# Halo of a causal convolution summed in one go, a softplus subtraction and one of sixteen state sums moved off VectorE

## The chip, the cores and the metric

One core of one Trainium2 chip. The metric is the device time in microseconds (us) of one execution, as the median of several runs. Engines are named as the profile names them: PE is TensorE (matmuls and transposes), DVE is VectorE, ACT is ScalarE, POOL is GpSimd, SP is SyncE, whose queue issues all the DMAs of this kernel.

## The reference, cut to what matters

The input is (4, 1024, 512) float32: 4096 tokens, handled in 8 chunks of 512 tokens, two chunks a sequence. Three residual blocks follow each other: half a gated feed-forward, a selective-scan block, half a gated feed-forward.

```python
x = x + 0.5 * ffn(_layernorm(x))
x = x + attn(_layernorm(x))          # W_in, causal conv of 4 taps, silu, Wx, softplus, scan, gate, Wout
x = x + 0.5 * ffn(_layernorm(x))

# inside attn, I = 1024 channels, N = 16 states
conv = causal_conv(h, conv_w)        # 4 taps along time: 3 tokens of the chunk before are needed
h = silu(conv + conv_b)
delta = softplus(dt + dt_bias)
s = exp(d_t * A) * s + d_t * B_t * u_t
y = sum over the 16 states n of s[n] * C_t[n]
```

## The kernel before, in words

**Layout.** Channels lie on the 128 partitions and 512 tokens on the free axis, so that the recurrence of one state over 128 channels is one scan instruction of DVE. The 1024 channels are 8 blocks (`NI`), handled in two groups of 4 (`ig`). Every matmul in float32 is split into a high and a low part (`split`, L499 by ACT for the high part, L500 by DVE or POOL for the low one).

**Stages of a chunk.** `ffn` is the feed-forward (gate and up matmuls L477, tanh L598, two products on DVE L600 and L608, down matmuls L548, `tail`). `prep_in` is the input projection with the convolution: for each block i, ACT writes tap 3 plus the bias from PSUM into `aa` (L652), DVE adds the taps k = 1, 2, 3 of the chunk's own tokens (L659), and where the chunk is the second of its sequence (odd c) each of these is followed by a small DVE operation that adds what tap k takes from the chunk before, 1, 2 or 3 elements wide, from `hsave` (L663). Even chunks save their last three columns into `hsave` (L656). ACT's tanh (L666) and DVE's product (L668) end the block. `softplus` works on two blocks at once (128x1024), in four parts a chunk: ACT computes exp(-abs(x)), 1 plus it, DVE the rounding error of that sum (L792), ACT the logarithm (L794), DVE subtracts the error (L796) and adds max(x, 0) (L800), POOL multiplies by u (L803). `post` reads y back, adds D*u, multiplies by the gate, and projects with Wout; its gate inputs are loaded into 6 slots, 3 of them in `aa`.

**The scan** of chunk c has 32 turns, 16 states n for each of the two groups. In a turn POOL multiplies `dus` by the broadcast row of B in two halves (L892, 128x1024) into one of 3 buffers `sbuf`; ACT computes four exponentials (L906) into 2 PSUM buffers `pa`; DVE runs four scans (L915) over the buffer in place; PE transposes the buffer in four steps tt of four 128x128 blocks (L932) into 2 PSUM banks `pt`; and each bank is multiplied by C and added to `acc` by one DVE operation (L943), apart from state 0, which ACT writes alone (L939). A bank of `pt` is free again when its reader is done, and a buffer of `sbuf` when its transposes are done.

**Order.** All instructions of the kernel are put in streams, and `merge` writes the order of each engine's queue in advance, from a model of durations (`span`) in which the stream that can start first goes first and `RANK` breaks near ties: the transposes and sums are thread T, the products, exponentials and scans are thread S (last in rank), softplus is D, the convolution is C. An engine works off its queue strictly in order, each instruction waiting for its semaphores. The rounds are `ffn1(c)`, `dt1(c-1)`, `post(c-3)` with `scan(c-3)`, `dt2`, `prep_in`, `dt3`, `ffn2(c-3)`, `dt0`, so that scans of older chunks fill the engines beside the projections of newer ones. y goes through memory, so the scan of a chunk isn't tied to its `post`. The weights of this input leave their low parts out in the feed-forwards (the light branch).

Of the kernel before, what the change touches and what calls it, by code (L numbers as in the profile page):

```python
# [7 lines left out]
P = 128  # L8
TC = 512
NCH = 8  # L10
H = 512
NI = 8
N = 16
J = 11
R = 128
HALO = 3
SLOTS = 3
DWELL = 12.0
ISSUE, LAND = 0.42, 2.5
LATE = {"pe": 0.3, "act": 0.08, "dve": 0.08, "pool": 0.1}  # L20
SLACK = 0.3
PEF = 1.0

# [6 lines left out]

RANK = {"z": {}, "l": dict(pe=0, act=0, dve=0, pool=0, slack=SLACK), "c": dict(act=1, dve=1, pool=1, slack=SLACK),
        "m": dict(pe=1, act=1, dve=1, pool=1, slack=SLACK), "d": dict(act=2, dve=2, pool=2, slack=SLACK),
        "t": dict(pe=0, dve=3, act=3), "s": dict(act=4, dve=4, pool=4)}

GU, DN, WIN, WO = 0, 2 * J, 3 * J, 3 * J + 16
NPIECE = 3 * J + 16 + 8
# [2 lines left out]
F32 = mybir.dt.float32  # L39
F32R = mybir.dt.float32r  # L40
ALU = mybir.AluOpType
# [143 lines left out]
def macaron(nc, x_in, wp_in, wx_in, wdt_in, const_in, lnw_in, ds_in, ident_in, out):  # L185
    ctx = ExitStack()
    with ctx:
        def sb(name, shape, dt=F32):
            return ctx.enter_context(nc.sbuf_tensor(name, shape, dt))
# [27 lines left out]
        xT = sb("xT", [P, 2, 4, TC], F32R)  # L217
        act = sb("act", [P, 2, J, TC], F32R)
        th = sb("th", [P, 2, TC])
        aa = sb("aa", [P, 3, TC])  # L220
        hd = sb("hd", [P, 3, TC])
        tb = sb("tb", [P, 8, TC])
        tsT = sb("tsT", [P, 2, TC], F32R)
# [9 lines left out]
        nb = sb("nb", [P, 4])  # L233
        mhalf = sb("mhalf", [P, 12])
        hsave = sb("hsave", [P, NI, 4])
        cst = sb("cst", [P, NCONST])
        csh = sb("csh", [P, 11 + 11 + 4 + 40])
        lnw = sb("lnw", [P, 2 * N])
# [33 lines left out]
        def ld(name, n=1):  # L272
            return [counter(f"{name}{i}") for i in range(n)]
# [1 line left out]
        l_const, l_w, l_wst = ld("l_const"), ld("l_w", SLOTS), ld("l_wst", 4)  # L275
        l_xn, l_x, st_x, st_xn = ld("l_xn")[0], ld("l_x")[0], ld("st_x")[0], ld("st_xn")[0]
        st_u, st_g, st_dl, l_u = ld("st_u", 2), ld("st_g", 2), ld("st_dl")[0], ld("l_u", 5)
        st_b, l_y, l_g = ld("st_b")[0], ld("l_y", 2), ld("l_g", 6)
        l_dl, l_du, l_b, st_y = ld("l_dl", 4), ld("l_du", 4), ld("l_b", 2), ld("st_y", 2)
        l_ud, st_du = ld("l_ud")[0], ld("st_du")[0]  # L280

# [126 lines left out]
        def build(light, first=False):  # L408
# [85 lines left out]
            def freed(name):  # L494
                return free.get(name, ())
# [89 lines left out]
            def ffn(one, c):  # L585
                s_in, s_out = (0, 1) if one else (2, None)
                if first:
                    t_xT = make_xT(t_xn0, tb)
                else:
                    t_xT = make_xT(xn_tok.pop((s_in, c)))  # L590
                    prefetch()
                a_tok = []
                for j in range(J):
                    r, q = j % 3, j % 2
                    slot, t_w = piece(GU + 2 * j)
                    b, w = bank()
                    t = gemm(b, slot, t_w, w, t_xT, 0 if light else None)
                    t_th = M.op("act", lambda e, b=b, q=q, j=j: e.activation(  # L598
                        th[:, q, :], pm[b][:, :], ACT.Tanh, scale=hc(H_GS + j)), t, *freed(("th", q)), table="tanh")
                    t_a = M.op("dve", lambda e, b=b, r=r, q=q: e.scalar_tensor_tensor(  # L600
                        aa[:, r, :], th[:, q, :], 1.0, pm[b][:, :], ALU.add, ALU.mult), t_th, *freed(("aa", r)))
                    free["th", q] = (t_a,)
                    bank_free[b] = (t_a,)
                    if not light:
                        slot, t_w = piece(GU + 2 * j + 1)
                    b, w = bank()
                    t = gemm(b, slot, t_w, w, t_xT, 1 if light else None)
                    t_h = M.op("dve", lambda e, b=b, r=r, j=j: e.scalar_tensor_tensor(  # L608
                        hd[:, r, :], aa[:, r, :], hc(H_US + j), pm[b][:, :], ALU.mult, ALU.mult),
                        t, t_a, *freed(("hd", r)))  # L610
                    bank_free[b] = (t_h,)
                    free["aa", r] = (t_h,)
                    t_hi, t_lo = split(hd[:, r, :], act[:, 0, j, :], act[:, 1, j, :], t_h, lo_eng="pool", waits=freed("act"))
                    free["hd", r] = (t_hi, t_lo)
                    a_tok.append((t_hi, t_lo))
                free["xT"] = (t,)
                if one:
                    tail(J, DN, None, a_tok, x_in, x2_d, 1, c)
                else:
                    tail(J, DN, None, a_tok, x3_d, out, None, c, last_out=True)  # L620
# [14 lines left out]
            def prep_in(c):  # L635
# [5 lines left out]
                    pre_norm(free, ln_out, c + 1)  # L641
                prefetch(0 if c == 0 else 1)
                u_tok, g_tok = [], []
                for i in range(NI):
                    r = i % 2
                    if c == 0 and light and i == NI - SLOTS + 1:
                        split_pieces(later)
                    slot, t_w = piece(WIN + i)
                    b, w = bank()
                    t = gemm(b, slot, t_w, w, t_xT)  # L650
                    cw = lambda k, i=i: hc(H_CW + 4 * i + k)
                    t_c = C.op("act", lambda e, b=b, r=r, i=i, cw=cw: e.activation(  # L652
                        aa[:, r, :], pm[b][:, :], ACT.Identity, bias=hc(H_CB + i), scale=cw(3)),
                        t, *freed(("aa", r)))
                    if even:
                        hs_tok[i] = C.op("dve", lambda e, b=b, i=i: e.tensor_copy(  # L656
                            hsave[:, i, 0:HALO], pm[b][:, TC - HALO:TC]), t_c, n=1)
                    for k in range(1, 4):
                        t_c = C.op("dve", lambda e, b=b, r=r, k=k, cw=cw: e.scalar_tensor_tensor(  # L659
                            aa[:, r, k:TC], pm[b][:, 0:TC - k], cw(3 - k), aa[:, r, k:TC], ALU.mult, ALU.add),  # L660
                            t_c)
                        if not even:
                            t_c = C.op("dve", lambda e, i=i, r=r, k=k, cw=cw: e.scalar_tensor_tensor(  # L663
                                aa[:, r, 0:k], hsave[:, i, HALO - k:HALO], cw(3 - k), aa[:, r, 0:k],
                                ALU.mult, ALU.add), t_c, hs_tok[i], n=1)
                    t_th = C.op("act", lambda e, b=b, r=r: e.activation(pm[b][:, :], aa[:, r, :], ACT.Tanh),  # L666
                                t_c, table="tanh")
                    t_u = C.op("dve", lambda e, b=b, r=r: e.scalar_tensor_tensor(  # L668
                        hd[:, r, :], pm[b][:, :], 1.0, aa[:, r, :], ALU.add, ALU.mult), t_th, *freed(("hd", r)))
                    free["aa", r] = (t_u,)  # L670
                    bank_free[b] = (t_u,)
                    t_hi = C.op("act", lambda e, r=r, i=i: e.activation(act[:, 0, i, :], hd[:, r, :], ACT.Copy),  # L672
                                t_u, *freed("act"))
                    t_lo = C.op("pool", lambda e, r=r, i=i: e.tensor_tensor(  # L674
                        act[:, 1, i, :], hd[:, r, :], act[:, 0, i, :], ALU.subtract), t_hi)
                    t_st = C.dma(st_u[r], u_d[c, i], hd[:, r, :], t_u)
                    u_tok.append(t_st)
                    free["hd", r] = (t_hi, t_lo, t_st)
                    if c and i < NI - 2:
                        g_tok.append(gate(c, i, t_xT))  # L680
# [91 lines left out]
            def softplus(c, part):  # L772
# [11 lines left out]
                if part == 3:  # L784
# [8 lines left out]
                    spw[:, :, :], spw[:, :, :], 1.0, spe[:, :, :], ALU.subtract, ALU.subtract), t_w, n=n)  # L793
                t_l = D.op("act", lambda e: e.activation(spe[:, :, :], spe[:, :, :], ACT.Ln, bias=1.0), t_q,  # L794
                           n=n, table="ln")
                t_l = D.op("dve", lambda e: e.tensor_tensor(spe[:, :, :], spe[:, :, :], spw[:, :, :], ALU.subtract),  # L796
                           t_l, n=n)
                t_u = D.dma(l_ud, spw[:, :, :], u_d[c, i0:i0 + 2].rearrange("k p n -> p k n"),
                            u_tok[i0], u_tok[i0 + 1], t_l)
# [12 lines left out]
            def post(c):  # L812
# [2 lines left out]
                a_tok = []  # L815
                ysb = xT[:, :, :, :].bitcast(F32)
                u_slot = [th[:, q, :] for q in range(2)] + [act[:, 0, k, :].bitcast(F32) for k in range(NI, J)]
                g_slot = [aa[:, q, :] for q in range(3)] + [act[:, 1, k, :].bitcast(F32) for k in range(NI, J)]
                u_free = [freed(("th", q)) for q in range(2)] + [freed("act")] * (J - NI)
                g_free = [freed(("aa", q)) for q in range(3)] + [freed("act")] * (J - NI)  # L820
                t_y = [M.dma(l_y[g], ysb[:, g, :, :], y_d[c * TC:(c + 1) * TC, g * 512:(g + 1) * 512].rearrange(
                    "(t p) n -> p t n", p=P), y_tok[g], *freed("xT")) for g in range(2)]
                for i in range(NI):
                    r, q, v = i % 3, i % 5, i % 6
                    t_u = M.dma(l_u[q], u_slot[q], u_d[c, i], u_tok[i], *u_free[q])
                    t_g = M.dma(l_g[v], g_slot[v], sg_d[c, i], g_tok[i], *g_free[v])
                    b, w = bank()
# [14 lines left out]
                free["xT"] = (t,)  # L842
                for q in range(2):
                    free["th", q] = u_free[q]
                for q in range(3):
                    free["aa", q] = g_free[q]
                tail(NI, WO, 0.5, a_tok, x2_d, x3_d, 2, c)

# [5 lines left out]
            def sf(name):  # L854
                return sfree.get(name, ())
# [5 lines left out]
            def scan(c):  # L861
# [22 lines left out]
                for g in range(2 * N):  # L884
# [43 lines left out]
                    for tt in range(4):  # L928
# [13 lines left out]
                        else:  # L942
                            f = lambda e, tt=tt, a=a, c=c, pb=pb, n=n: e.scalar_tensor_tensor(  # L943
                                a, pt[pb][:, :], cT[:, c % 4, tt, n:n + 1], a, ALU.mult, ALU.add)
                            w = sf(("accw", ig, tt))
                        t_a = T.op("act" if n == 0 else "dve", f, t_t, t_ct, *w)
                        sfree["accw", ig, tt] = (t_a,)
                        sfree["pt", pb] = (t_a,)
                    sfree["sb", s3] = (t_t, t_c)
                    if n == N - 1:  # L950
                        t_s = T.dma(st_y[ig], y_d[c * TC:(c + 1) * TC, ig * 512:(ig + 1) * 512].rearrange(
# [184 lines left out]
```

How the kernel before makes its waits and increments, by code:

```python
def play(eng, items, passed):  # L173
    for waits, fn, sem, _ in items:
        for counter, value in waits:
            if passed.get(counter, 0) < value:
                passed[counter] = value
                eng.wait_ge(counter.handle, value)
        ins = fn(eng)
        if sem is not None:
            ins.then_inc(sem[0].handle, sem[1])
# [877 lines left out]
        def run(e, name):  # L1060
            passed = {}
            play(e, setup_order.get(name, []), passed)
            e.wait_ge(t_flag[0].handle, t_flag[1])
            v = e.value_load(flag[0:1, 0:1].bitcast(mybir.dt.int32))
            with e.If(v == 0):
                play(e, orders[True][0][name], dict(passed))
                if name == "sp":
                    for c, n in orders[True][1]:
                        e.wait_ge(c.handle, n)
            with e.Else():
                play(e, orders[False][0][name], dict(passed))
                if name == "sp":
                    for c, n in orders[False][1]:
                        e.wait_ge(c.handle, n)
```

## Time and profile before

| | us |
|---|---|
| median of 3 runs | 3351.01 (3345.28 to 3353.27) |
| the profiled execution, its own time | 3343.89 |
| its span, from the first to the last instruction | 3342.1 |
| DVE busy | 2855.8 (85% of the span) |
| PE busy | 2507.3 (75%) |
| POOL busy | 1823.7 (55%) |
| ACT busy | 1580.7 (47%) |

The profile is of one execution. Its page gives busy time by engine, the span in 40 slices, the chain of work that ended last, and groups of instructions by source line with their busy time, their mean and what ended the idle time before them. Views of the trace behind it give the same for a stretch of time, for one line (with the shortest, median and longest instruction), the waits of one engine for another, and the instructions in order of time.

### The profile page before, as it was taken

To read this page: it belongs to the slowest core of one execution; us is meant where nothing else is said; L and a number is where in the kernel's file an instruction comes from. 1 tells how busy PE (TensorE), PEld (TensorE's weight loads), DVE (VectorE), ACT (ScalarE), POOL (GpSimd) and SP (SyncE) were. 2 spreads that over 40 slices of the span, in tenths; PEclk is the share of its full clock that TensorE was granted. 3 is DMA by queue.
4 is the path that set the end of the run, shared out by engine and by line. 5 is a ranking of instruction groups with operands and counts; after the bars stand their busy time and mean duration, and the time that the engine had idled before them with its cause. 6 is when DMAs were issued, how large, how long until landed. Compare 5 with 4: busy or idle time off the path is not lost. (4 is left out here: it accounts for less than half of the span.)

```text
span 3342.1 us, 36946 instructions
## 1 busy us (share of the span) xinstructions
PE 2507.3 (75%) x12266; PEld 2033.2 (61%) x12266; DVE 2855.8 (85%) x3661; ACT 1580.7 (47%) x2637; POOL 1823.7 (55%) x951
## 2 busy tenths in 40 slices
PE   7467667677876898788875998778875877769557
PEld 6346556556665776577664776567664755557346
DVE  5628989699998998899998999989999998899942
ACT  4435345456554554455543554555544546344312
POOL 2216545355744676456744666457744675656612
PEclk9768878788887998889887998889887988879668
DMA  7844542653763466745764467745764465545333
GB/s 268 314 159 132 178 173 96 198 202 124 271 238 117 145 224 236 250 141 170 259 238 132 138 208 262 249 138 161 246 233 139 134 232 193 202 156 183 107 111 114
DMA packets 301078, 624.41 MB, mean 187 GB/s; under 512 B 23504, under 2 KB 24272, under 8 KB 300880
## 3 DMA queue, kind: packets, MB, share of 16 engines
q1 hardware_dynamic: 300880, 621.96, 55.6%
q8 instruction: 101, 1.65, 0.2%
q14 instruction: 97, 0.79, 0.1%
HBM read 466.15 MB, written 155.71 MB: 186 GB/s over the span
## 5 line engine op out<-in xcount | busy, mean ns | idle before, releaser
L892 POOL TENSOR_TENSOR sbuf<-dus,bring 128x1024 f32<-128x1024 f32 x512 | 1223.7, 2410 | 824.1 <-PE pt L932 727.3
L477 PE MATMUL pm<-xT,wring 128*128 128x512 f32 x4352 | 1175.4, 421 | 228.5 <-DVE hd L668 113.3
L477 PEld LDWEIGHTS pm<-xT,wring 128*128 128x128 f32 x4352 | 847.9, 202 | 431.3 <-issue 251.8
L906 ACT ACTIVATE pa<-dls,cst 128x512 f32<-128x512 f32 x1024 | 695.0, 688 | 746.3 <-DVE sbuf L915 744.8
L932 PE MATMUL pt<-ident,sbuf 128*128 128x128 f32 x4096 | 689.3, 312 | 327.4 <-DVE sbuf L915 283.0
L932 PEld LDWEIGHTS pt<-ident,sbuf 128*128 128x128 f32 x4096 | 559.3, 161 | 469.9 <-DVE sbuf L915 317.1
L943 DVE SCALAR_TENSOR_TENSOR acc<-pt,cT,acc 128x512 f32<-128x512 f32 x960 | 692.6, 743 | 167.2 <-PE pt L932 160.7
L915 DVE TENSOR_TENSOR_SCAN sbuf<-pa,carry,sbuf 128x512 f32<-128x512 f32 x512 | 634.2, 1267 | 13.9 <-ACT pa L906 13.8
L548 PE MATMUL pm<-wring,act 128*128 128x512 f32 x2176 | 591.9, 417 | 51.2 <-DVE aa L600 24.6
L915 DVE TENSOR_TENSOR_SCAN sbuf<-pa,sbuf 128x512 f32<-128x512 f32 x512 | 605.4, 1209 | 11.6 <-ACT pa L906 7.8
L548 PEld LDWEIGHTS pm<-wring,act 128*128 128x128 f32 x2176 | 411.3, 197 | 150.0 <-DVE aa L600 27.4
L500 POOL TENSOR_TENSOR act<-hd,act 128x512 fp32r<-128x512 f32 x240 | 323.8, 1353 | 307.1 <-ACT act L499 300.9
L499 ACT ACTIVATE act<-hd 128x512 fp32r<-128x512 f32 x240 | 149.8, 627 | 216.0 <-DVE hd L608 149.1
L600 DVE SCALAR_TENSOR_TENSOR aa<-th,pm 128x512 f32<-128x512 f32 x176 | 117.6, 668 | 35.8 <-ACT th L598 35.1
L477 PE MATMUL pm<-wxs,act 128*128 128x160 f32 x768 | 113.2, 309 | 42.5 <-POOL act L674 42.5
L659 DVE SCALAR_TENSOR_TENSOR aa<-pm,csh,aa 128x511 f32<-128x511 f32 (+2 forms) x192 | 141.1, 735 | 0.9
L674 POOL TENSOR_TENSOR act<-hd,act 128x512 fp32r<-128x512 f32 x64 | 82.0, 1281 | 105.1 <-ACT act L672 100.5
L608 DVE SCALAR_TENSOR_TENSOR hd<-aa,csh,pm 128x512 f32<-128x512 f32 x176 | 128.9, 732 | 10.7 <-PE pm L477 10.2
L598 ACT ACTIVATE th<-pm,csh 128x512 f32<-128x512 f32 x176 | 118.8, 675 | 39.1 <-PE pm L477 38.5
L477 PEld LDWEIGHTS pm<-wxs,act 128*128 128x128 f32 x768 | 107.3, 224 | 44.5 <-issue 44.5
L803 POOL TENSOR_TENSOR spw<-spx,spw 128x1024 f32<-128x1024 f32 x32 | 76.1, 2378 | 91.7 <-DMA spw<-u_d 84.3
L923 ACT ACTIVATE carry<-sbuf 128x4 f32<-128x4 f32 x128 | 26.6, 208 | 188.5 <-DVE sbuf L915 188.4
(92 smaller groups left out, 1843.6 us busy)
## 6 DMA issues: line engine op xcount, KB each, us to landing
wring<-wsp SPq DMA_DIRECT2D x424, 512.0 KB, 3.9
bring<-b_d SPq DMA_DIRECT2D x256, 256.0 KB, 3.9
xn_d<-tb SPq DMA_DIRECT2D x24, 1024.0 KB, 9.5
xnb<-xn_d SPq DMA_DIRECT2D x22, 1024.0 KB, 7.0
x_d<-tb SPq DMA_DIRECT2D x16, 1024.0 KB, 5.5
u_d<-hd SPq DMA_DIRECT2D x64, 256.0 KB, 3.4
spw<-u_d SPq DMA_DIRECT2D x32, 512.0 KB, 4.1
dl_d<-spx SPq DMA_DIRECT2D x32, 512.0 KB, 6.3
```

The lines of the kernel that those rows point to most:

```text
L477: f = lambda e, pw=pw, px=px, k=k, first=(i == 1), end=(i == total): e.matmul(pm[b][:, 0:n], lhs(pw, k), rhs(px, k), start=first, stop=end)
L499: t_hi = M.op(hi_eng, lambda e: e.activation(hi, b_or_src, ACT.Copy), t_src, *waits)
L500: t_lo = M.op(lo_eng, lambda e: e.tensor_tensor(lo, b_or_src, hi, ALU.subtract), t_hi)
L548: f = lambda e, b=b, pw=pw + half, px=px, k=k, tt=tt, slot=slot, start=(i and k == 0), stop=(end and k == nk - 1): e.matmul(pm[b][:, :], a ...
L598: t_th = M.op("act", lambda e, b=b, q=q, j=j: e.activation(th[:, q, :], pm[b][:, :], ACT.Tanh, scale=hc(H_GS + j)), t, *freed(("th", q)), ...
L608: t_h = M.op("dve", lambda e, b=b, r=r, j=j: e.scalar_tensor_tensor(hd[:, r, :], aa[:, r, :], hc(H_US + j), pm[b][:, :], ALU.mult, ALU.mul ...
L659: t_c = C.op("dve", lambda e, b=b, r=r, k=k, cw=cw: e.scalar_tensor_tensor(aa[:, r, k:TC], pm[b][:, 0:TC - k], cw(3 - k), aa[:, r, k:TC], ...
L892: t_p = S.op("pool", lambda e, s2=s2, s3=s3, h=h: e.tensor_tensor(sbuf[:, s3, h * m:(h + 1) * m, :], dus[:, h * m:(h + 1) * m, :], bring[: ...
L906: t_e = S.op("act", lambda e, k=k, i=i, pb=pb, n=n: e.activation(pa[pb][:, :], dls[:, k, :], ACT.Exp, scale=col(C_A + i * N + n)), dl_tok[ ...
L915: t_sc = S.op("dve", lambda e, d=d, pb=pb, init=init: e.tensor_tensor_scan(d, pa[pb][:, :], d, init, ALU.mult, ALU.add), t_e, t_ps[k], *(s ...
L932: f = lambda e, tt=tt, k=k, s3=s3, pb=pb: e.matmul(pt[pb][:, k * P:(k + 1) * P], sbuf[:, s3, k, tt * P:(tt + 1) * P], ident[:, :], is_tran ...
L943: f = lambda e, tt=tt, a=a, c=c, pb=pb, n=n: e.scalar_tensor_tensor(a, pt[pb][:, :], cT[:, c % 4, tt, n:n + 1], a, ALU.mult, ALU.add)
```

## The change

- In odd chunks `prep_in` first computes on POOL, for all 8 blocks at once, what the three taps take from `hsave`: three small multiplications and two small additions into `hfix` (128x8x3 at most). Each block then gets one DVE addition of 3 columns right after L652, in place of the three operations L663. `hsave` isn't overwritten before POOL has read it.
- The subtraction of softplus (L796) runs on POOL.
- The sum over the states for n = 8 isn't done by DVE: ACT multiplies the bank of `pt` by C into a buffer `tmp`, and POOL adds `tmp` to `acc`. There is one `tmp`, so ACT's next multiplication waits for POOL's addition. The bank is free after ACT.
- The room for `tmp` comes from `aa`, which has 2 buffers instead of 3; `ffn` alternates between two, and `post` has 5 slots for the gate inputs instead of 6.

```diff
+SHARED = (8,)
-        "t": dict(pe=0, dve=3, act=3), "s": dict(act=4, dve=4, pool=4)}
+        "t": dict(pe=0, dve=3, act=3, pool=3), "s": dict(act=4, dve=4, pool=4)}
...
-        aa = sb("aa", [P, 3, TC])
+        aa = sb("aa", [P, 2, TC])
+        tmp = sb("tmp", [P, 1, TC])
...
+                if not even:
+                    cw4 = csh[:, H_CW:H_CW + 4 * NI].rearrange("p (i k) -> p i k", k=4)
+                    at = {3: 0, 2: 4, 1: 6}
+                    for k in (3, 2, 1):
+                        t_fix = C.op("pool", lambda e, k=k: e.tensor_tensor(
+                            hfix[:, :, at[k]:at[k] + k], hsave[:, :, HALO - k:HALO],
+                            cw4[:, :, 3 - k:4 - k].broadcast_to([P, NI, k]), ALU.mult),
+                            *(hs_tok if k == 3 else ()), *freed("hfix"), n=8)
+                    for k in (2, 1):
+                        t_fix = C.op("pool", lambda e, k=k: e.tensor_tensor(
+                            hfix[:, :, 0:k], hfix[:, :, 0:k], hfix[:, :, at[k]:at[k] + k], ALU.add), t_fix, n=8)
+                    free["hsave"] = (t_fix,)
...
-                            hsave[:, i, 0:HALO], pm[b][:, TC - HALO:TC]), t_c, n=1)
+                            hsave[:, i, 0:HALO], pm[b][:, TC - HALO:TC]), t_c, *freed("hsave"), n=1)
+                    else:
+                        t_c = C.op("dve", lambda e, i=i, r=r: e.tensor_tensor(
+                            aa[:, r, 0:HALO], aa[:, r, 0:HALO], hfix[:, i, 0:HALO], ALU.add), t_c, t_fix, n=1)
+                        free["hfix"] = (t_c,)
...
-                        if not even:
-                            t_c = C.op("dve", lambda e, i=i, r=r, k=k, cw=cw: e.scalar_tensor_tensor(
-                                aa[:, r, 0:k], hsave[:, i, HALO - k:HALO], cw(3 - k), aa[:, r, 0:k],
-                                ALU.mult, ALU.add), t_c, hs_tok[i], n=1)
...
-                t_l = D.op("dve", lambda e: e.tensor_tensor(spe[:, :, :], spe[:, :, :], spw[:, :, :], ALU.subtract),
+                t_l = D.op("pool", lambda e: e.tensor_tensor(spe[:, :, :], spe[:, :, :], spw[:, :, :], ALU.subtract),
...
-                    r, q, v = i % 3, i % 5, i % 6
+                    r, q, v = i % 3, i % 5, i % 5
...
+                        if n in SHARED:
+                            t_s = T.op("act", lambda e, tt=tt, c=c, pb=pb, n=n: e.activation(
+                                tmp[:, 0, :], pt[pb][:, :], ACT.Copy, scale=cT[:, c % 4, tt, n:n + 1]),
+                                t_t, t_ct, *sf("tmp"))
+                            t_a = T.op("pool", lambda e, a=a: e.tensor_tensor(a, a, tmp[:, 0, :], ALU.add), t_s, *w)
+                            sfree["tmp"] = (t_a,)
+                            sfree["pt", pb] = (t_s,)
+                        else:
+                            t_s = t_a = T.op("act" if n == 0 else "dve", f, t_t, t_ct, *w)
+                            sfree["pt", pb] = (t_a,)
                         sfree["accw", ig, tt] = (t_a,)
-                        sfree["pt", pb] = (t_a,)
```

## Rows read from the trace of the kernel before

**Rows 1.** The page, its first part: busy time, share, instructions.

```profile
PE 2507.3 (75%) x12266; PEld 2033.2 (61%) x12266; DVE 2855.8 (85%) x3661; ACT 1580.7 (47%) x2637; POOL 1823.7 (55%) x951
```

**Rows 2.** Busy time by stretch, all engines; the first line names the columns.

```profile
core 0: us, PE busy (x) PEld busy (x) DVE busy (x) ACT busy (x) POOL busy (x), PEclk, DMA share, GB/s
0.00:300.00 300.00, 184.85 (x761) 150.57 (x762) 157.91 (x276) 139.11 (x234) 80.27 (x52) 0.79 0.64 228
300.00:1600.00 1300.00, 1010.21 (x5052) 820.65 (x5051) 1174.79 (x1506) 644.42 (x1104) 748.76 (x385) 0.87 0.55 183
1600.00:2900.00 1300.00, 1019.43 (x5097) 825.69 (x5095) 1200.17 (x1497) 652.13 (x1079) 783.98 (x405) 0.88 0.59 197
2900.00:3206.00 306.00, 202.27 (x968) 161.53 (x968) 290.31 (x333) 122.62 (x187) 185.44 (x91) 0.73 0.42 140
3206.00:3342.00 136.00, 90.58 (x392) 74.76 (x392) 32.67 (x53) 22.38 (x34) 25.26 (x20) 0.83 0.42 138
```

**Rows 3.** Waits of one engine for another: us in total, times, longest.

```profile
DVE acc L943 <- PE pt L932: 158.0, 168, 4.0
...
POOL sbuf L892 <- PE pt L932: 727.3, 172, 12.3
...
ACT pa L906 <- DVE sbuf L915: 744.8, 577, 9.4
```

**Rows 4.** Groups by line and shape, the DVE work removed: busy us, mean ns.

```profile
L943 DVE SCALAR_TENSOR_TENSOR acc<-pt,cT,acc 128x512 f32<-128x512 f32 x960 | 692.6, 743 | 167.2 <-PE pt L932 160.7
...
L796 DVE TENSOR_TENSOR spe<-spe,spw 128x1024 f32<-128x1024 f32 x32 | 50.2, 1568 | 2.6 <-ACT spe L794 2.6
...
L663 DVE SCALAR_TENSOR_TENSOR aa<-hsave,csh,aa 128x3 f32<-128x3 f32 x32 | 32.2, 1007 | 0.0
...
L663 DVE SCALAR_TENSOR_TENSOR aa<-hsave,csh,aa 128x1 f32<-128x1 f32 x32 | 16.1, 504 | 0.1
L663 DVE SCALAR_TENSOR_TENSOR aa<-hsave,csh,aa 128x2 f32<-128x2 f32 x32 | 16.0, 501 | 0.1
```

**Rows 5.** Busy time of line L796 alone, between 300 and 3206 us.

```profile
300.00:3206.00 2906.00, 43.89 (x28) 0.86 0.56 185
```

**Rows 6.** Single lines: shortest, median and longest instruction in ns.

```profile
L663 DVE SCALAR_TENSOR_TENSOR aa<-hsave,csh,aa x96: 188/213/2434, 409.8 to 2580.2; 128x1 f32<-128x1 f32 x32, 128x2 f32<-128x2 f32 x32, 128x3 f32<-128x3 f32 x32
...
L796 DVE TENSOR_TENSOR spe<-spe,spw x32: 1193/1216/3339, 200.1 to 2802.2; 128x1024 f32<-128x1024 f32 x32
...
L800 DVE SCALAR_TENSOR_TENSOR spx<-spx,spe x32: 1206/1225/3245, 201.3 to 2806.7; 128x1024 f32<-128x1024 f32 x32
...
L943 DVE SCALAR_TENSOR_TENSOR acc<-pt,cT,acc x960: 714/744/754, 269.5 to 3205.6; 128x512 f32<-128x512 f32 x192
```

**Rows 7.** Timeline near 1017 us: start, duration, engine, line.

```profile
1017.32 4.65 POOL L892 TENSOR_TENSOR sbuf<-dus,bring 128x1024 f32<-128x1024 f32 x2 [6.95 <-PE pt L932]
...
1017.86 1.83 DVE L663 SCALAR_TENSOR_TENSOR aa<-hsave,csh,aa 128x3 f32<-128x3 f32 x1
```

**Rows 8.** Groups by line and shape nearest to the work added.

```profile
L892 POOL TENSOR_TENSOR sbuf<-dus,bring 128x1024 f32<-128x1024 f32 x512 | 1223.7, 2410 | 824.1 <-PE pt L932 727.3 <-DMA dus<-du_d 43.9 <-issue 39.9
...
L564 POOL TENSOR_TENSOR tb<-tb 128x512 f32<-128x512 f32 x64 | 80.1, 1281 | 52.8 <-DVE tb L562 52.8
...
L800 DVE SCALAR_TENSOR_TENSOR spx<-spx,spe 128x1024 f32<-128x1024 f32 x32 | 56.2, 1757 | 0.4
...
L939 ACT ACTIVATE acc<-pt,cT 128x512 f32<-128x512 f32 x64 | 41.7, 683 | 10.9 <-PE pt L932 5.7 <-DMA y_d<-acc 4.8
...
L313 POOL TENSOR_TENSOR rs<-ve,mhalf 128x4 f32<-128x4 f32 x24 | 28.9, 1203 | 104.0 <-DVE ve L312 103.6
```

**Rows 9.** Timeline of DVE near 3110 us, where scans run alone.

```profile
3110.73 1.61 DVE L943 SCALAR_TENSOR_TENSOR acc<-pt,cT,acc 128x512 f32<-128x512 f32 x2
...
3118.40 0.75 DVE L943 SCALAR_TENSOR_TENSOR acc<-pt,cT,acc 128x512 f32<-128x512 f32 x1
```

More of the change, by code:

```diff
@@ L235, in macaron @@
         hsave = sb("hsave", [P, NI, 4])
+        hfix = sb("hfix", [P, NI, 8])
         cst = sb("cst", [P, NCONST])
@@ L277, in macaron @@
         st_u, st_g, st_dl, l_u = ld("st_u", 2), ld("st_g", 2), ld("st_dl")[0], ld("l_u", 5)
-        st_b, l_y, l_g = ld("st_b")[0], ld("l_y", 2), ld("l_g", 6)
+        st_b, l_y, l_g = ld("st_b")[0], ld("l_y", 2), ld("l_g", 5)
         l_dl, l_du, l_b, st_y = ld("l_dl", 4), ld("l_du", 4), ld("l_b", 2), ld("st_y", 2)
@@ L599, in ffn @@
                         th[:, q, :], pm[b][:, :], ACT.Tanh, scale=hc(H_GS + j)), t, *freed(("th", q)), table="tanh")
-                    t_a = M.op("dve", lambda e, b=b, r=r, q=q: e.scalar_tensor_tensor(
-                        aa[:, r, :], th[:, q, :], 1.0, pm[b][:, :], ALU.add, ALU.mult), t_th, *freed(("aa", r)))
+                    t_a = M.op("dve", lambda e, b=b, q=q: e.scalar_tensor_tensor(
+                        aa[:, q, :], th[:, q, :], 1.0, pm[b][:, :], ALU.add, ALU.mult), t_th, *freed(("aa", q)))
                     free["th", q] = (t_a,)
@@ L607, in ffn @@
                     t = gemm(b, slot, t_w, w, t_xT, 1 if light else None)
-                    t_h = M.op("dve", lambda e, b=b, r=r, j=j: e.scalar_tensor_tensor(
-                        hd[:, r, :], aa[:, r, :], hc(H_US + j), pm[b][:, :], ALU.mult, ALU.mult),
+                    t_h = M.op("dve", lambda e, b=b, r=r, q=q, j=j: e.scalar_tensor_tensor(
+                        hd[:, r, :], aa[:, q, :], hc(H_US + j), pm[b][:, :], ALU.mult, ALU.mult),
                         t, t_a, *freed(("hd", r)))
                     bank_free[b] = (t_h,)
-                    free["aa", r] = (t_h,)
+                    free["aa", q] = (t_h,)
                     t_hi, t_lo = split(hd[:, r, :], act[:, 0, j, :], act[:, 1, j, :], t_h, lo_eng="pool", waits=freed("act"))
@@ L817, in post @@
                 u_slot = [th[:, q, :] for q in range(2)] + [act[:, 0, k, :].bitcast(F32) for k in range(NI, J)]
-                g_slot = [aa[:, q, :] for q in range(3)] + [act[:, 1, k, :].bitcast(F32) for k in range(NI, J)]
+                g_slot = [aa[:, q, :] for q in range(2)] + [act[:, 1, k, :].bitcast(F32) for k in range(NI, J)]
                 u_free = [freed(("th", q)) for q in range(2)] + [freed("act")] * (J - NI)
-                g_free = [freed(("aa", q)) for q in range(3)] + [freed("act")] * (J - NI)
+                g_free = [freed(("aa", q)) for q in range(2)] + [freed("act")] * (J - NI)
                 t_y = [M.dma(l_y[g], ysb[:, g, :, :], y_d[c * TC:(c + 1) * TC, g * 512:(g + 1) * 512].rearrange(
@@ L844, in post @@
                     free["th", q] = u_free[q]
-                for q in range(3):
+                for q in range(2):
                     free["aa", q] = g_free[q]
@@ L945, in scan @@
                             w = sf(("accw", ig, tt))
-                        t_a = T.op("act" if n == 0 else "dve", f, t_t, t_ct, *w)
+                        if n in SHARED:
[8 more added lines that the diff above has]
+                            sfree["pt", pb] = (t_a,)
                         sfree["accw", ig, tt] = (t_a,)
-                        sfree["pt", pb] = (t_a,)
                     sfree["sb", s3] = (t_t, t_c)
```

## The prediction

> **What bounds the kernel now.** I read four views in this order. The page's first part comes first: DVE is busy 85% of the span, PE 75%, POOL 55%, ACT 47% [rows 1]. An average hides the opening and the end, so the second view is busy time by stretch [rows 2]. In the first 300 us DVE is busy only 158, since the scans have nothing to work on yet; in the last 136 us, after the last scan, it is busy 33. Between 300 and 3206 us it is busy 1174.8 + 1200.2 + 290.3 = 2665 of 2906 us, 91.7%, and idle for 241. PE has 2232 us of work in the same stretch (77%) and POOL 1718 (59%). Third come the waits [rows 3]: ACT's exponentials wait 745 us for DVE's scans and POOL's products 727 us for buffers that come free only after DVE and PE, so both stand behind DVE. DVE itself waits mostly for the transposes ahead of its sums, 158 us in 168 waits of 1 us or so. Last, a stretch with scans alone [rows 9]: one turn takes 3118.40 - 3110.73 = 7.67 us, which is four scans and four sums of DVE back to back. So from 300 to 3206 us the length is DVE's work plus a twelfth, and the 136 us behind it are a chain that the change hardly touches. Scans have the lowest rank and fill what is left of DVE, so work that leaves DVE anywhere in these 2906 us should let them end earlier.
>
> **What sets the price of small operations.** The halo operation L663 works on 1 to 3 columns and has a median of 213 ns, but means of 504, 501 and 1007 ns and a longest of 2434 [rows 4, 6]. The timeline shows why [rows 7]: POOL starts two products at 1017.32, 4.65 us together, and L663, started at 1017.86, ends at 1019.69, where the first product ends (1017.32 + 2.33). The same is seen for L796 and L800, with medians of 1.22 us and longest of 3.2 to 3.3 [rows 6]. All these read both their inputs in SBUF. The sums L943, with one input in PSUM, never take over 754 ns [rows 6], though POOL is busy more than half of the time. So a DVE operation with two SBUF inputs that starts beside a POOL operation stands still until that ends, and the others don't notice POOL.
>
> **The change part by part.** (1) Halo. Removed are 32.2 + 16.1 + 16.0 = 64.3 us of DVE [rows 4], all within the bound stretch. Added are 4 odd chunks x 8 blocks = 32 additions of 3 columns, again with both inputs in SBUF. Bounds: 0.19 us each (the shortest L663 [rows 6]) and 1.01 (the mean of the 3-column form [rows 4]); I take the mean of all three forms, 0.67, since the new place, behind ACT's first tap, has no tie to POOL's products: 32 x 0.67 = 21.4 us, between 6 and 32. POOL's 4 x 5 = 20 small operations have no twin; the small power operation takes 1.20 us [rows 8], so at most 24 us of POOL. They need only the halo of the chunk before and are hidden by the transposes and matmuls ahead of the first tap; without that cover the first block of each odd chunk waits 5 x 1.2 us, 24 us in all, and I take none. The new waits on `hsave` are for work of a chunk earlier: nothing.
>
> (2) Softplus. Of 50.2 us of L796, 43.9 lie in the bound stretch [rows 4, 5]; the other 6.3 lie in the opening, where DVE idles. POOL takes it at 2.41 us (the product of the same shape [rows 8]), 1.2 more than DVE's median, so the path logarithm, subtraction, sum, product gets longer; in the opening two such parts stand before the first scan, +3 us. New is that L800 waits, in order on DVE, for POOL, and that POOL may go straight on to its next product when L800 becomes ready. Today L800 pays a mean of 1.76 against a median of 1.23, so 0.53 of waiting [rows 6, 8]; waiting for a whole product each time would be 2.41 - 0.53 = 1.9 more. Bounds for 28 parts: 0 and 53 us; I take 0.5 each, as the mean wait of L663 (0.67 - 0.2) shows for an operation that meets POOL by chance, 14 us. Behind a late L800 everything of DVE queues; for POOL coming later than the planned order assumes I take 0.3 us each, 8 us (0 to 28 x 2.4 = 67, if a whole product stands ahead each time).
>
> (3) State 8. Removed are 64 of 960 sums at 692.6 / 960 = 0.72 us, 46.2 us [rows 4]. ACT gets 64 x 0.68 = 44 us (the same form in L939) and POOL 64 x 1.28 = 82 us (as L564) [rows 8]; both have room, ACT at 47% and POOL at 55% [rows 1]. The four steps of a turn run in series through the one `tmp`: 4 x (0.68 + 1.28) = 7.9 us, and with two products, 4.8 us, let into POOL's gaps, 12.7. State 9's transposes need the banks in the meantime, so its sums come late, but three buffers of `sbuf` let DVE scan states 9 and 10 first: 8 scans, which by rows 9 fill at least 2 x (7.67 - 4 x 0.72) = 9.6 us, and outside the last stretch other work beside them. Cover and chain are nearly equal, so I charge 1 us in each of 16 turns, 16 us, between -10 (the waits for transposes, 158 x 64 / 960, go too [rows 3, 4]) and the full 12.7 a turn, 203.
>
> (4) POOL's load in the bound stretch rises from 1718 by 28 x 2.41 + 82 + 20 = 169 us, a tenth. The waits of all DVE operations with two SBUF inputs grow likewise; the three softplus lines and small operations hold some 50 us of such waiting, so 5 us. `aa` with two buffers costs nothing: its reader L608 is on the same engine and ready first. Five gate slots match the five slots for u: nothing.
>
> **The sum.** Relief of DVE in the bound stretch: 64.3 + 43.9 + 46.2 = 154.4. Less 21.4, 14 and 5: 114. Not all of it becomes time: where DVE was 91.7% busy I let that share hold, 105 us. Less 16 and 8 for new stalls and 3 in the opening: 78 us. The profiled execution took 3343.9, so 3266; the median lies 7 us above it, so 3273 us, 2.3% faster.
>
> A page speaks against parts (1) and (2). The Trainium skill (SBUF — State Buffer, Who interferes with whom) says that the pair of ports shared by DVE and GpSimd is locked for a whole instruction, and that a DVE operation with two SBUF inputs is blocked by a GpSimd one that reads SBUF; rows 7 agree to 0.04 us. And the Trainium skill (Perfetto Trace Analysis, Optimizing Scalar/DVE Operations) warns that moving work between these two engines might therefore not help. That is the first rival.
>
> **Rivals.** *Lock.* The freed time of (1) and (2) goes back as waiting: the halo addition at 32, L800 at 53. Relief is 154.4 - 32 - 53 - 5 = 64, times 0.917 = 59, less 27: 32 us faster, 3319. For it speaks that POOL's next product is often ready at once; against it that POOL waits 727 us for buffers [rows 3], so it often has nothing ready. 0.13.
>
> *PE takes over.* PE has 77% of the bound stretch, and its queue is in order too, so part of DVE's new free time is spent waiting for transposes and matmuls. If half of the 105 goes that way: 53 - 27 = 26 us faster, 3325. For it speak the 158 us that DVE waits for transposes [rows 3]; against it that 23% of PE is open. 0.13.
>
> *The chain of state 8 (slower).* If DVE stands for the whole of it, 12.7 us in 16 turns, 203 us: 105 - 203 - 11 = 109 slower, 3460. Place: the one `tmp` between ACT and POOL, with ACT's exponentials queued behind a multiplication that waits for it, and scans behind those. It decides from (105 - 11) / 16 = 5.9 us a turn. For it speaks the in-order queue of ACT; against it the 9.6 us of scans that are ready. 0.11.
>
> **How the numbers follow.** The forecast, 60 to 115 us faster, has 0.50; lock 0.13; PE 0.13; more than the forecast (stalls at their lower bounds: 154.4 - 6 = 148) 0.06; nothing to be seen 0.07; slower 0.11. Faster by over 0.3% (about what a measurement of this kernel can tell from no change) is 0.50 + 0.13 + 0.13 + 0.06 = 0.82, within it 0.07, slower 0.11. The range reaches from 3220, most of the way to the lower bounds, to 3350, which takes in both milder rivals and leaves out the slower one.
>
> **What would show it.** DVE's busy time should fall by about 120 us to some 2740, with 896 sums L943, 32 halo additions of about 0.67 us and L800 at 2.0 to 2.5 us on average; L800 at 3 us would show the lock rival. DVE's idle time in the bound stretch should grow by some 35 us at most; growing waits for PE show the second rival. In the turns of state 8, waits of DVE's scans for ACT or POOL over 5.9 us would show the third. The prediction is wrong if DVE's busy time falls as said and the end does not move with it.

## The result and the profile after

| | before | changed |
|---|---|---|
| median, us | 3349.99 (4 runs) | 3260.3 (4 runs, 3256.42 to 3261.99) |
| ratio | | 0.9732 (95% interval 0.9715 to 0.9749) |
| profiled execution, its own time | 3343.89 | 3256.42 |
| its span | 3342.1 | 3254.6 |

The changed kernel is 2.7% faster, 90 us; 3273 us was forecast. Its page, first part (compare [rows 1]):

```profile
PE 2479.2 (76%) x12266; PEld 2009.1 (62%) x12266; DVE 2751.5 (85%) x3501; ACT 1619.1 (50%) x2701; POOL 1981.0 (61%) x1067
```

DVE has 104 us less to do, with 160 instructions fewer, and its share of the span is 85% as before: the span shrank with the work. The bound stretch ends at 3117 us instead of 3206. Busy time in the bound stretch, in the columns of [rows 2]:

```profile
300.00:3117.00 2817.00, 2202.94 (x11137) 1783.97 (x11135) 2570.35 (x3182) 1459.67 (x2439) 1868.47 (x988) 0.88 0.57 191
```

In it DVE is busy 2570 us against 2665 (95 less) and idle 247 against 241. Nearly all of DVE's relief became time. Groups by line, to be read beside [rows 4] and [rows 8]; the lines are numbered anew, L958 was L943, L815 was L800, L811 was L796:

```profile
L958 DVE SCALAR_TENSOR_TENSOR acc<-pt,cT,acc 128x512 f32<-128x512 f32 x896 | 642.9, 741 | 130.8 <-PE pt L947 125.0
...
L965 POOL TENSOR_TENSOR acc<-acc,tmp 128x512 f32<-128x512 f32 x64 | 85.0, 1328 | 77.1 <-ACT tmp L962 77.1
...
L815 DVE SCALAR_TENSOR_TENSOR spx<-spx,spe 128x1024 f32<-128x1024 f32 x32 | 70.7, 2208 | 20.3 <-POOL spe L811 20.3
...
L674 DVE TENSOR_TENSOR aa<-aa,hfix 128x3 f32<-128x3 f32 x32 | 21.5, 671 | 0.2 <-ACT aa L667 0.2
```

The halo addition L674 takes 671 ns on average, and L815 takes 0.45 us more than L800 did. New is the wait of L815 for POOL's subtraction, 20 us in all. DVE's waits in the bound stretch (us in total, times, longest):

```profile
DVE acc L958 <- PE pt L947: 120.9, 127, 5.1
DVE sbuf L930 <- ACT pa L921: 32.3, 38, 3.8
DVE spx L815 <- POOL spe L811: 15.4, 11, 3.2
```

The wait for transposes fell from 158 to 121 us [rows 3], that for the exponentials rose from 21 to 32, and the one for POOL is new. The new waits, 26 us, are paid for by an old one that is 37 us smaller.

### The profile page after: what moved, and what is told of

It is laid out like the page before. It is cut to its first block and busy times, and to the rows that moved or that the text cites. A ratio compares the mean times of both kernels' runs of the same rounds, so it can differ in the third digit from the quotient of the medians.

```text
span 3254.6 us, 37061 instructions
## 1 busy us (share of the span) xinstructions
PE 2479.2 (76%) x12266; PEld 2009.1 (62%) x12266; DVE 2751.5 (85%) x3501; ACT 1619.1 (50%) x2701; POOL 1981.0 (61%) x1067
## 5 line engine op out<-in xcount | busy, mean ns | idle before, releaser
L480 PE MATMUL pm<-xT,wring 128*128 128x512 f32 x4352 | 1149.3, 415 | 175.0 <-DVE xT L503 83.4
L480 PEld LDWEIGHTS pm<-xT,wring 128*128 128x128 f32 x4352 | 838.6, 199 | 372.5 <-issue 197.8
L947 PE MATMUL pt<-ident,sbuf 128*128 128x128 f32 x4096 | 681.2, 308 | 334.7 <-DVE sbuf L930 234.6
L947 PEld LDWEIGHTS pt<-ident,sbuf 128*128 128x128 f32 x4096 | 545.0, 158 | 483.2 <-DVE sbuf L930 274.2
L958 DVE SCALAR_TENSOR_TENSOR acc<-pt,cT,acc 128x512 f32<-128x512 f32 x896 | 642.9, 741 | 130.8 <-PE pt L947 125.0
L930 DVE TENSOR_TENSOR_SCAN sbuf<-pa,carry,sbuf 128x512 f32<-128x512 f32 x512 | 633.6, 1267 | 16.6 <-ACT pa L921 16.1
L551 PE MATMUL pm<-wring,act 128*128 128x512 f32 x2176 | 588.8, 414 | 55.9 <-DVE hd L850 28.1
L811 POOL TENSOR_TENSOR spe<-spe,spw 128x1024 f32<-128x1024 f32 x32 | 76.2, 2380 | 96.6 <-ACT spe L809 96.4
L965 POOL TENSOR_TENSOR acc<-acc,tmp 128x512 f32<-128x512 f32 x64 | 85.0, 1328 | 77.1 <-ACT tmp L962 77.1
```

The source lines that it names most:

```text
L480: f = lambda e, pw=pw, px=px, k=k, first=(i == 1), end=(i == total): e.matmul(pm[b][:, 0:n], lhs(pw, k), rhs(px, k), start=first, stop=end)
L551: f = lambda e, b=b, pw=pw + half, px=px, k=k, tt=tt, slot=slot, start=(i and k == 0), stop=(end and k == nk - 1): e.matmul(pm[b][:, :], a ...
L930: t_sc = S.op("dve", lambda e, d=d, pb=pb, init=init: e.tensor_tensor_scan(d, pa[pb][:, :], d, init, ALU.mult, ALU.add), t_e, t_ps[k], *(s ...
L947: f = lambda e, tt=tt, k=k, s3=s3, pb=pb: e.matmul(pt[pb][:, k * P:(k + 1) * P], sbuf[:, s3, k, tt * P:(tt + 1) * P], ident[:, :], is_tran ...
```

## The experiments

All ratios are to the kernel before, run on the same chip in the same job, with their 95% intervals.

**One part alone, three kernels.** First the halo: `hfix` on POOL and one addition on DVE, all else as before.

```diff
+    # on POOL, for all 8 blocks: hfix = three multiplications and two additions (shortened)
+    aa[:, r, 0:3] += hfix[:, i, 0:3]          # DVE, once a block
-    L663, three times a block
```

> The kernel before with the halo part alone (summed by POOL, one addition a block on DVE). Theory of the sum: DVE loses 64.3 us and gets 32 additions of about 0.67 us, a relief of 43 us, of which 92% become time: 39 us faster, some 3311 (ratio 0.988). Lock rival: the addition costs 1 us each, and the added POOL work gives some back: 25 to 28 us faster (0.992). If the halo sat beside DVE's path: no change.

Measured: 3292.79 us, ratio 0.9846 (0.9825 to 0.9866), 51 us faster, more than the 39 expected, and the lock rival's 28 is out. In its bound stretch (300 to 3155 us) DVE is busy 2619.4 us, 46 less, and idle 236, 5 less.

The softplus subtraction alone:

```diff
-    t_l = D.op("dve", ... spe - spw)
+    t_l = D.op("pool", ... spe - spw)
```

> The kernel before with the softplus subtraction alone on POOL. Theory of the sum: 43.9 us of DVE leave the bound stretch, L800 gets 0.45 us slower (14 us), DVE waits some 15 us for POOL's subtraction, 3 us go in the opening: 10 to 15 us faster (ratio 0.996). Lock rival: L800 and the waits eat all of it, 0 to 10 us slower (1.000 to 1.003).

Measured: 3332.76 us, ratio 0.9962 (0.9947 to 0.9977), 13 us faster, as the sum had it; the lock rival's loss did not come. Its L800, which reads both inputs in SBUF and now follows POOL's subtraction, shows what meeting POOL costs:

```profile
L800 DVE SCALAR_TENSOR_TENSOR spx<-spx,spe 128x1024 f32<-128x1024 f32 x32 | 72.9, 2278 | 16.8 <-POOL spe L796 16.7
```

50 us of work left DVE; 17 came back as a longer L800 (56.2 before [rows 8]) and 17 as waiting for POOL. In the bound stretch (300 to 3195 us) DVE is busy 30 us less (2635.6) and idle 259, 19 more.

State 8 alone, with the smaller rings that it needs:

> The kernel before with the sum of state 8 alone moved (ACT multiplies, POOL adds; aa with two buffers, five gate slots). With the stalls that the prediction charged, 1 us a turn: 27 us faster (ratio 0.992). With the chain fully covered by the scans of the next states: 42 to 50 us faster (0.986). With the whole chain exposed, 12.7 us a turn: 160 us slower (1.048).

Measured: 3332.71 us, ratio 0.9964 (0.9954 to 0.9974), 12 us faster. That is less than either covered case. 46 us of sums left DVE, but in the bound stretch it is busy only 27 less (2638.0) and idle 256, 15 more. Part of the missing relief is in the profile: the halo operations, L663 in the kernel before, here L666, have become longer (67.5 us in place of 64.3) and so has L317, L314 in the kernel before, by 8 us. That POOL's heavier load is the reason was not tested. The lengthening isn't uniform either: of L666 the 3-column form grew from 32.2 us to the 38.7 below, the 1-column form fell from 16.1 to 9.3.

```profile
L666 DVE SCALAR_TENSOR_TENSOR aa<-hsave,csh,aa 128x3 f32<-128x3 f32 x32 | 38.7, 1210 | 0.0
```

**Do the smaller rings cost anything?** `aa` with two buffers and five gate slots, nothing else changed.

> The kernel before with two buffers of aa and five gate slots, and nothing else of the change. Prediction: costs nothing, ratio 1.000 (0.998 to 1.002). Rival for why state 8 alone gave 13 us and not 27: the smaller rings cost some 15 us, ratio 1.004 or more.

Measured: 3349.28 us, ratio 1.0000 (0.9991 to 1.0009). They cost nothing that can be seen, so the shortfall of state 8 alone lies in the move itself.

**Leave one part out.** The changed kernel without state 8 (`SHARED = ()`), and with the softplus subtraction back on DVE.

> The changed kernel with state 8 back on DVE (halo and softplus parts, small rings). If the parts add up: 0.985 + 0.996 - 1 = 0.981, some 3282. If they help each other (DVE idles less when two parts are in) the ratio is below 0.979. The difference to the changed kernel (0.973) is what state 8 gives beside the others: 0.004 as alone, or up to 0.014 as the sum of its 46 us would have it.

> The changed kernel with the softplus subtraction back on DVE (halo and state 8 parts). Alone the softplus part gave 0.4%; if the parts add up this kernel stands at 0.985 + 0.996 - 1 = 0.981, and if softplus is worth more beside the others, above 0.981.

Measured: 3282.55 us, ratio 0.9800 (0.9783 to 0.9816), and 3279.07 us, ratio 0.9797 (0.9784 to 0.9810). Beside the other parts state 8 is worth 0.9800 - 0.9732 = 0.7% and softplus 0.9797 - 0.9732 = 0.65%, against 0.4% each alone. The three parts alone add up to 1.5 + 0.4 + 0.4 = 2.3%, together they give 2.7%. For each of the two the difference is about as large as the intervals together, so that they help each other is likely and not certain. Two parts in one kernel show nothing of it: halo with softplus stands at 0.9800 and halo with state 8 at 0.9797, where the parts alone add up to 0.981. DVE's idle time in the bound stretch says where the gain of the third part lies: 259 us with softplus alone, 256 with state 8 alone, 260 with halo and softplus, 250 with halo and state 8, and 247 with all three. State 8, added last, takes 17 us of busy time and 13 us of idle time away. Why the idle time falls is open.

**Is it the shared port that makes the small addition long?** In the changed kernel the addition is rewritten so that one input comes from PSUM: POOL adds the bias to `hfix` too, and DVE computes the three columns from the matmul's bank.

```diff
-    aa[:, r, 0:3] = aa[:, r, 0:3] + hfix[:, i, 0:3]
+    aa[:, r, 0:3] = pm[b][:, 0:3] * cw(3) + hfix[:, i, 0:3]
```

> The changed kernel, but the halo addition reads the block's first three columns from PSUM (times tap 3) and adds hfix, into which POOL has also summed the bias: one SBUF input instead of two. If the shared port is what makes the addition take 0.67 us: every one of the 32 takes 0.13 to 0.25 us, none over 0.4, and DVE gets 14 to 16 us of relief, ratio 0.968 to 0.970 against 0.973. If its length has another cause (the width, the wait for ACT): it stays near 0.6 us and the time the same.

Measured: 3247.26 us, ratio 0.9692 (0.9676 to 0.9708). The line in the changed kernel and in this one (shortest, median and longest in ns):

```profile
L674 DVE TENSOR_TENSOR aa<-aa,hfix x32: 123/606/2234, 410.6 to 2491.6; 128x3 f32<-128x3 f32 x32
```

```profile
L678 DVE SCALAR_TENSOR_TENSOR aa<-pm,csh,hfix x32: 180/194/221, 405.8 to 2481.0; 128x3 f32<-128x3 f32 x32
```

The width, the place in the queue and the wait for ACT are the same, and POOL is as busy (1865 us of the bound stretch). The operation is another one (a product and an addition), but the three L663 of the kernel before were of that kind too and took up to 2434 ns [rows 6]. What is left is that one input has moved from SBUF to PSUM, and the longest falls from 2234 to 221 ns. DVE's relief in the bound stretch is 19 us. By the medians 13 us of it became time, by the profiled runs 9; the intervals of the two ratios leave room for 6 to 21.

**How far can the states go?** `SHARED = (4, 8, 12)` and `SHARED = (2, 4, 6, 8, 10, 12)` in the changed kernel.

> The changed kernel with the sums of states 4, 8 and 12 moved instead of 8 alone: DVE loses another 92 us, POOL gets another 164 us (74% busy in the bound stretch), ACT 88. If the chain through the one tmp is covered in every turn and POOL's load doesn't matter: another 70 to 90 us faster, about 3180 (0.949). If POOL's load lengthens DVE's operations with two SBUF inputs and its queue comes late: 20 to 50 us faster than the changed kernel, about 3225. If the chain starts to show: no further gain or a loss.

> The changed kernel with the sums of states 2, 4, 6, 8, 10 and 12 moved. Two further states gave 60 us; three more would give another 90 if the trade went on as it did (0.928). POOL would then be busy some 2270 us of a bound stretch of 2660, 85%, and its queue, in order, carries products, additions and subtractions: if it becomes late, DVE's waits for POOL and ACT grow and the gain falls to 0.935 to 0.955 or turns back.

Measured: 3192.06 us, ratio 0.9550 (0.9533 to 0.9567), and 3179.08 us, ratio 0.9497 (0.9483 to 0.9512). The first is 68 us faster than the changed kernel by the medians (61 by the ratios), short of the 70 to 90 expected for a chain that is covered in every turn; the second lies where it was put if POOL becomes late. By the ratios the second and third state bring 30 us each, the next three 6 us each. With six states the bound stretch reads:

```profile
300.00:3039.00 2739.00, 2206.04 (x11118) 1793.20 (x11116) 2381.43 (x2861) 1636.38 (x2750) 2269.04 (x1305) 0.87 0.59 196
```

DVE is busy 2381 us and idle 358, where it idled 247 with one state and 271 with three (2748 - 2477). The relief still comes, 96 us from three states to six, and nearly all of it turns into idle time. POOL's timeline in that kernel, near 3015 us:

```profile
3011.00 1.28 POOL L965 TENSOR_TENSOR acc<-acc,tmp 128x512 f32<-128x512 f32 x1
3012.22 2.38 POOL L907 TENSOR_TENSOR sbuf<-dus,bring 128x1024 f32<-128x1024 f32 x1
3014.53 1.30 POOL L965 TENSOR_TENSOR acc<-acc,tmp 128x512 f32<-128x512 f32 x1
3015.76 2.37 POOL L907 TENSOR_TENSOR sbuf<-dus,bring 128x1024 f32<-128x1024 f32 x1
3018.07 1.29 POOL L965 TENSOR_TENSOR acc<-acc,tmp 128x512 f32<-128x512 f32 x1
```

From 3000.39 us on, for 28 us, POOL has no gap: a product of 2.4 us stands between any two additions, so a step takes 3.5 us. With every second state moved, two turns hold four products and four additions of POOL, 14 us, while DVE's work for them is eight scans and four sums, about 12.5 us (9.6 from [rows 9], as the prediction took them, and 4 x 0.72). There POOL's own work is longer than DVE's. ACT's multiplications wait for POOL:

```profile
ACT tmp L962 <- POOL acc L965: 153.9, 157, 3.3
```

In the changed kernel that wait is 26.9 us in 25 waits, with three states 67.8 in 78. Per addition it is 0.42, 0.35 and 0.40 us with one, three and six states, so the chain through `tmp` gets no longer for each turn. Two causes fit the idle time, then: more turns with a chain, and a POOL without slack (83% of the bound stretch, 74% with three states). DVE's own waits from three states to six grow by 22 us for transposes, 32 for exponentials and 19 for POOL's products. A kernel with two `tmp` buffers would tell the causes apart; it was not run.

**Both together.** The halo addition from PSUM with states (4, 8, 12), (3, 6, 9, 12) and the six states.

> States 4, 8 and 12 moved, and the halo addition with one SBUF input. The two gains are for different reasons and should add: 0.955 - 0.004 = 0.951, and no halo addition over 0.4 us though POOL is busy 74% of the bound stretch.

> States 3, 6, 9 and 12 moved, and the halo addition with one SBUF input. With three states DVE idled 271 us in the bound stretch, with six 358. If four turns of sixteen still leave the chain covered: 30 us less than with three, 0.943. If the chain already shows as with six: 0.945 to 0.950.

> States 2, 4, 6, 8, 10 and 12 moved, and the halo addition with one SBUF input. If with six states the order of work through tmp and POOL is the bound and not DVE's work, 18 us less DVE work bring little: 0.949. If DVE still bounds most of it: 0.945.

Measured: 3179.46 us, ratio 0.9502 (0.9487 to 0.9516); 3174.17 us, 0.9484 (0.9469 to 0.9498); 3166.79 us, 0.9452 (0.9414 to 0.9489). The addition from PSUM gives its 0.4 to 0.5% with one state, with three and, by the median, with six, so even there DVE's work still sets part of the time; the interval of the last ratio nearly reaches the 0.949 of the other case. With the states 3, 6, 9 and 12 in place of 4, 8 and 12 the gain is 0.2%, 6 us, where a covered chain would have given 30: DVE is busy 21 us less (2435), with 64 sums fewer, and idles 299 us instead of 277. The last kernel is the fastest seen, 5.5% below the kernel before and 2.9% below the changed one, though its interval overlaps those of the other two.

## Why the prediction held, point by point

**What bounds the kernel.** The reading that the stretch from 300 to 3206 us is DVE's work plus a constant idle share held in the main, and is the step on which the rest stood. Across the kernels before, with halo alone and as changed, DVE's busy time there goes 2665, 2619, 2570 us, and the stretch's length 2906, 2855, 2817. It holds less well for the small parts: with softplus alone DVE is busy 30 us less and the stretch 11 shorter, with state 8 alone 27 and 12. The idle share is not constant. Idle time lies between 236 and 260 us in the kernels with at most one state moved, a spread as large as one small part is worth. The end, 137 us after the last sum, did not move.

**What the operations stand still for.** The prediction said that DVE operations with two SBUF inputs stand still beside POOL and "the others don't notice". The second half is too wide. It looked at the sums, which read PSUM. In the kernel before, operations with a single tensor input, in SBUF, stand still as well:

```profile
L312 DVE TENSOR_SCALAR ve<-mv x24: 138/170/2118, 13.6 to 3246.2; 128x4 f32<-128x4 f32 x24
```

The longest starts at 1326.85, beside a product of POOL that started at 1326.60, and ends at 1328.97, where the product ends (1326.60 + 2.35). The same is seen for L737, with a median of 281 ns and a longest of 2459.

**Part 1, halo.** Price of the new addition: 0.67 us taken, 0.671 measured. That it fits so well is in part luck: the same addition takes 0.74 us on average with halo alone, 0.48 without state 8, 0.76 without the softplus part and 0.80 with three states. POOL's small operations, bounded by 1.2 us, take 0.23 (the median). What the sum left out: the three L663 stood in a row of dependent operations whose end PE waits for, since the last product of the block frees its bank. PE's waits, before and with the halo part alone:

```profile
PE pm L477 <- DVE hd L668: 113.3, 38, 7.8
```

```profile
PE pm L478 <- DVE hd L681: 50.1, 26, 4.3
```

They are more than halved, DVE's idle time in the stretch did not grow at all, and the part gave 51 us where the sum's share of it was 39. That the shorter row is the reason for the whole of the 12 us was not tested by itself. Against it speaks that the addition from PSUM shortens the row again and PE's waits for it stay as they are (55.9 us in the changed kernel, 58.1 there).

**Part 2, softplus.** L800 was put at 0.5 us more and got 0.45. The waits for POOL were put at 8 us (bounds 0 and 67) and are 15 in the bound stretch. The part alone gave 13 us; by its terms (43.9 less 14, times 0.917, less 8 and 3) it would have been 16.

**Part 3, state 8.** ACT's 0.68 us and POOL's 1.28 were met (0.685, and 1.29 as a median; the mean is 1.33, since three additions take over 2 us, each beside a DVE operation with two SBUF inputs, as below in the section on the hardware). The chain through `tmp` was put at 7.9 to 12.7 us and judged covered by DVE's scans of states 9 and 10. The last such turn of the changed kernel, DVE alone, from the first multiplication at 3062.71 to the last addition's end at 3073.93, 11.2 us:

```profile
3059.06 4.80 DVE L930 TENSOR_TENSOR_SCAN sbuf<-pa,carry,sbuf 128x512 f32<-128x512 f32 x4
3064.01 4.81 DVE L930 TENSOR_TENSOR_SCAN sbuf<-pa,carry,sbuf 128x512 f32<-128x512 f32 x4 [0.16 <-ACT pa L921]
3068.74 0.72 DVE L958 SCALAR_TENSOR_TENSOR acc<-pt,cT,acc 128x512 f32<-128x512 f32 x1
3069.38 2.45 DVE L930 TENSOR_TENSOR_SCAN sbuf<-pa,carry,sbuf 128x512 f32<-128x512 f32 x2
3072.39 1.60 DVE L958 SCALAR_TENSOR_TENSOR acc<-pt,cT,acc 128x512 f32<-128x512 f32 x2 [0.56 <-PE pt L947]
```

Seven scans and three sums fill it, and 0.7 us stay idle, about the 1 us charged. That is one turn. By itself the part gave 12 us where the sum's terms gave 27, and it is the term that the sum had most wrong; beside the other two it gave 23. With six states DVE's idle time grows by 87 us over three states, as shown above, but whether by the rival's chain or by POOL's load is open.

**The sum.** Relief in the bound stretch was put at 114 us and is 95; DVE's idle time was let grow by 33 and grew by 6. The two misses offset each other, so it is in part luck that the forecast came within 13 us of the median. The parts show the same: alone, halo gave 12 us more than its share, state 8 15 us less, and together the three gave 14 us more than alone. The smaller relief has two sources. I added up durations of groups, and these overlap: group by group DVE's work falls by 118 us in the whole span, but the page's busy time, which counts an overlap once, by 104. Two instructions back to back share about 0.1 us, and 160 are gone. And the operations that stand still beside POOL grew by more than the 5 us allowed (the small ones of the norms, L312, L314 and L737, by 5 us each), though L792 fell by 7. The idle time that hardly grew: I charged the idle share and the new stalls on top of each other, while the waits above show new stalls in the place of old ones; with halo alone DVE's idle time fell by 5 us.

**The rivals.** Lock: L815 at 3 us was its mark, it is 2.2. PE takes over: the waits for transposes fell. The chain of state 8: covered at one state in the turn shown; at six states not told apart from POOL's load.

## What to carry to other kernels

Where one engine is busy over 90% of a stretch and the others wait for it, price an edit as that engine's work, expect an error of some 20 us in 3300 from the idle time, and take the page's busy time, not the sum of means, for what it holds. Small operations are priced by what they wait for and not by their width (0.67 us on average for 3 columns here, 0.20 with an input from PSUM): give a VectorE operation one input from PSUM where GpSimd is busy, even if a product has to be computed twice. Work handed to a slower engine through one buffer can be hidden where the first engine has other work for the length of the chain, but not all of the relief becomes time (12 of 46 us alone, 30 of 46 at best). Count the idle time, and the slower engine's own load, as the number of such turns grows.

## What the runs showed of the hardware

A DVE operation with two SBUF inputs stands still beside a POOL operation (2234 ns at worst for 3 columns), and with one of its inputs from PSUM it doesn't (221 ns at worst). This agrees with the Trainium skill (SBUF — State Buffer, Who interferes with whom). Operations with one tensor input, in SBUF, stood still too (L312, 2118 ns at worst).

It works the other way too: POOL's addition L965 takes 1286 ns by the median and 2304 at most. The longest starts 0.04 us behind a DVE operation with two SBUF inputs, and ends 1.13 us after it:

```profile
765.71 1.21 DVE L807 SCALAR_TENSOR_TENSOR spw<-spw,spe 128x1024 f32<-128x1024 f32 x1
765.75 2.30 POOL L965 TENSOR_TENSOR acc<-acc,tmp 128x512 f32<-128x512 f32 x1 [4.92 <-ACT tmp L962]
```

The DVE operation came first and took its usual time, and POOL's took its own time after it.

Not expected was how little the warning that moves between the two might not help (the Trainium skill, Perfetto Trace Analysis, Optimizing Scalar/DVE Operations) weighed here: of the 50 us of the moved subtraction, 17 came back as blocking and 17 as waiting, and 13 us were gained.
